# Router logits of three batches from one fp32 sum, added up on GpSimd in two halves of the tokens, in place of TensorE products of two parts

## The chip, the cores and the metric

The kernel runs on one core of one Trainium2 chip. Its time is the time of the device in microseconds (us); lower is better. Engines are named as the profile names them: PE is TensorE (PEld its loading of weights), DVE is VectorE, ACT is ScalarE, POOL is GpSimd, SP is SyncE.

## The reference

A gated block over 4 batches of 512 tokens of width 512: cross attention to 512 context rows of width 128, then a mixture of experts beside a shared network, both on a layer norm of the running x. Everything is fp32.

```python
x = x + tanh(g_xattn[0]) * xattn(layernorm(x), ctx_512, W_k, b_k, ln_gamma, ln_beta)
x = x + tanh(g_ffn[0]) * ffn(layernorm(x), gate_w, e_bias, Wu, Wd, Wsu, Wsd)

def ffn(h, ...):                      # h: 2048 x 512
    logits = h @ gate_w               # 512 x 32: this is what the change is about
    scores = sigmoid(logits)          # then groups, top 2 of 4 groups, top 4 of 32 experts, weights
    ...
    routed = sum over the 4 chosen experts of w * relu2(h @ Wu[e]) @ Wd[e]
    return routed + relu2(h @ Wsu) @ Wsd
```

The logits decide which experts a token gets, so they are computed in full fp32.

## The kernel before

The kernel is written engine by engine, each engine's instructions in an order set by hand, with semaphores between them. There is no scheduler: what stands first on an engine runs first.

The span has a front part (to about 136 us), where attention, the normalised rows `HR` and the shared network's products of the four batches b = 0 to 3 are interleaved; a middle part, where the shared network goes on beside the choice of experts; a loop over 81 expert tiles; and a tail that adds the experts' rows.

What the change touches lies in the front part. For each batch:
- DVE makes `HR` (`h_norm`, L1147) with a reciprocal root that POOL computes (`roots`, L592, an instruction of 128x4). PE turns `HR` (`h_t`, L1963), a tile of 128 tokens at a time.
- ACT copies a turned tile from PSUM into `hT_hi` as fp32r, the high part (L737). DVE subtracts that from the same PSUM tile, which gives `hT_lo`, the low part (`h_low`, L1152).
- The shared network's products (`up_shared`, `down_shared`) are each made of three: high by high, high by low, low by high, in fp32r (L1805).
- The logits (`logits_t`) are fp32 products of `gate` with `hT_hi` and then with `hT_lo`, both added in one PSUM bank. `gate` has 4 blocks of 128 rows by 32 experts, and block h writes its own 32 partitions of the bank, so that the four blocks lie in four column groups of PE. The bank `U[1]` then holds four partial sums; ACT copies it to `lgT`, PE turns that (`logits`, L1997), and DVE adds the four parts up into `LG` (L1160).
- Batch 3 is different: its logits come from the turned fp32 rows themselves. The change leaves it alone.

`U[1]` is shared. The next batch's `out_t` or `ctx_t` writes it, and so waits until DVE has read the logits out of it:

```python
            def out_t(b, js=range(TPB)):
                if js[0] == 0:
                    pe.wait_ge(s["act_kv"], b + 1)
                    if b == 3:
                        pe.wait_ge(s["dve_lg"], 2)
```

In DVE's order `logits(1)` stands behind the last `added` (L1130) and `x2_part` (L1135) of batch 2. DVE's instructions of the attention are `scaled` (L1112), `shifted` (L1118) and `added` (L1130); from batch 2 on `scaled` reads its scores from the SBUF tile `PS`, before that from PSUM. `low_part` (L1178) is the low part of the shared network's activations. POOL's whole list in the front part is its constants, `gam` and `bet`, and eight `roots`, two for each batch.

Of the kernel before, what the change touches and what calls it, by code (L numbers as in the profile page):

```python
# [5 lines left out]
P = 128  # L6
N_BATCH, SEQ, H = 4, 512, 512
DC = 128
TPB = SEQ // P
NT = N_BATCH * TPB  # L10
HB = H // P
E, INNER = 32, 256
# [22 lines left out]
def block_kernel(nc, x, ctx_in, g_xattn, g_ffn, w_k, b_k, ln_gamma, ln_beta,  # L35
                 gate_w, e_bias, w_up, w_down, w_sh_up, w_sh_down, out):
    f32, i32, u32 = mybir.dt.float32, mybir.dt.int32, mybir.dt.uint32
    f16, bf16, f32r = mybir.dt.float16, mybir.dt.bfloat16, mybir.dt.float32r
    ALU, ACT, AX = mybir.AluOpType, mybir.ActivationFunctionType, mybir.AxisListType
    ds = bass.ds  # L40

    with ExitStack() as stack:
        def sb(name, shape, dt=f32):
            return stack.enter_context(nc.sbuf_tensor(name, shape, dt))

        def bank(name):
            return stack.enter_context(nc.psum_tensor(name, [P, 512], f32))

        def sem(name):
            return stack.enter_context(nc.semaphore(name))  # L50
# [13 lines left out]
        gate = sb("gate", [P, HB, E])  # L64
# [56 lines left out]
        def at(name, shape, where, dt=f32):  # L121
            return where.enter_context(nc.sbuf_tensor(name, shape, dt))

        with ExitStack() as front:
            with ExitStack() as ramp:
                out2 = at("out2", [DC, 2, SEQ], ramp)
                key2 = at("key2", [DC, 2, SEQ], ramp)
            hT_hi = at("hT_hi", [P, 2, HB, SEQ], front, f32r)
            hT_lo = at("hT_lo", [P, 2, HB, SEQ], front, f32r)
            wsu_hi = at("wsu_hi", [P, HB, SI], front, f32r)  # L130
            wsd_hi = at("wsd_hi", [P, SB, H], front, f32r)
            spare = at("spare", [P, 2, HB, P], front)
            act_hi = at("act_hi", [P, A_SLOTS, SEQ], front, f32r)
            with ExitStack() as whole:
                wsu = at("wsu", [P, HB, SI], whole)
                wsd = at("wsd", [P, SB, H], whole)
                act = at("act", [P, A_SLOTS, SEQ], whole)
            wsu_lo = at("wsu_lo", [P, HB, SI], front, f32r)
            wsd_lo = at("wsd_lo", [P, SB, H], front, f32r)
            act_lo = at("act_lo", [P, A_SLOTS, SEQ], front, f32r)  # L140
            with ExitStack() as attention:
                ctx_b = at("ctx_b", [P, TPB, DC], attention)
                ctxT = at("ctxT", [DC, SEQ], attention)
                keyT = at("keyT", [DC, SEQ], attention)
                kv = at("kv", [P, TPB, DC], attention)
                PS = at("PS", [P, 2, TPB, SEQ], attention)
                pT = at("pT", [P, TPB, SEQ], attention)
                outT = ctxT
                wk = at("wk", [P, DC], attention)
                wkT = at("wkT", [P, DC], attention)  # L150
                bk = at("bk", [DC, 1], attention)
                gam = at("gam", [P, SEQ], attention)
                bet = at("bet", [P, SEQ], attention)
            with ExitStack() as route:
                with ExitStack() as end:
                    wsd_t = at("wsd_t", [P, SB, H], end)
                wu = at("wu", [P, W_SLOTS, HB, INNER], route)
                wd = at("wd", [P, W_SLOTS, IB, H], route)
                with ExitStack() as weighed:
                    yp2 = at("yp2", [P, 2, H], weighed)  # L160
                sc = at("sc", [P, NT, E], route)
                place = at("place", [P, E, NT], route)
                top_s = at("top_s", [P, NT, 8], route)
                sp_i = at("sp_i", [P, 3, NT, TOPK], route, u32)
                sp_f = at("sp_f", [P, 2, NT, TOPK], route)
                with ExitStack() as choice:
                    sfc = at("sfc", [P, NT, E], choice)
                    pair = at("pair", [P, 2, NT * GROUPS, EG // 2], choice)
                    four = at("four", [P, 4, NT * GROUPS, EG // 4], choice)
                    gsm = at("gsm", [P, 4, NT * GROUPS], choice)  # L170
                    gcmp = at("gcmp", [P, 2, NT, GROUPS, GROUPS], choice)
                    sm = at("sm", [P, NT, E + 4], choice)
                    sm2 = at("sm2", [P, NT, E + 4], choice)
                    top8 = at("top8", [P, NT, 8], choice)
                    chosen = at("chosen", [P, E, NT], choice, bf16)
                    run = at("run", [P, E, NT], choice)
                    incl = at("incl", [P, E, NT], choice)
                    n_i = at("n_i", [P, 2, E], choice, i32)
                with ExitStack() as found:
                    tsum = at("tsum", [P, N_TILES], found)  # L180
                    tpos = at("tpos", [P, TOPK, N_TILES], found)
                    tofs = at("tofs", [P, 2, N_TILES], found)
                with ExitStack() as kept:
                    with ExitStack() as whole:
                        wsu_t = at("wsu_t", [P, HB, SI], whole)
                    wsu_tlo = at("wsu_tlo", [P, HB, SI], kept, f32r)
                    with ExitStack() as matched:
                        yp3 = at("yp3", [P, 2, H], matched)
                    match = at("match", [P, NT // 4, TOPK, E], kept)
                selA = at("selA", [P, NT * TOPK // 2, P], route, f16)  # L190
                selB = at("selB", [P, NT * TOPK // 2, N_TILES], route, f16)
        wu2 = wu[:, :, :, :].rearrange("p s h n -> p (s h n)")
        wd2 = wd[:, :, :, :].rearrange("p s h n -> p (s h n)")
        with ExitStack() as early:
# [78 lines left out]
        U = [bank("U0"), bank("U1")]  # L273
# [29 lines left out]
        def outs_of(b):  # L303
            return out2[:, b, :] if b < 2 else outT[:, :]

        names = """d_x00 d_small d_gate d_tanh d_wk d_bk d_h d_out
            pool_c pool_r dve_c dve_wh pe_bk pe_g act_bk act_th
            dve_v dve_u dve_z dve_e dve_x1 dve_h dve_ws dve_lo dve_sh dve_hT dve_lg dve_ch
            dve_M dve_tab dve_sel dve_tabT dve_idx dve_eact dve_xl dve_el dve_wu dve_wd dve_cmb
            act_c act_ctxT act_kvT act_kv act_pT act_mean act_outT act_ss act_sim act_e act_r act_hT act_lgT act_ws act_sq act_sc  # L310
# [6 lines left out]
        s = {n: sem(n) for n in names}  # L317
# [241 lines left out]
        def _(pool):  # L559
# [29 lines left out]
            def roots(j, n):  # L589

                pool.wait_ge(s["dve_v"], n)
                pool.tensor_tensor(rstd[:, j, :], veps[:, j, :], mhalf[:, :], ALU.pow).then_inc(s["pool_r"], 1)  # L592

            pool.wait_ge(s["d_small"], 16 * 2)
            pool.tensor_scalar(gam[:, :], gam[:, :], -1.0, 0.0, ALU.mult, ALU.add).then_inc(c, 1)
            pool.tensor_scalar(bet[:, :], bet[:, :], -1.0, 0.0, ALU.mult, ALU.add).then_inc(c, 1)
            roots(0, 1)
            roots(1, 2)
            roots(0, 3)
            roots(1, 4)  # L600
            for b in range(2, N_BATCH):
                roots(0, 2 * b + 1)
                roots(1, 2 * b + 2)

            pool.wait_ge(s["dve_tab"], 2)
            used = pool.value_load(used_tab[0:1, 0:1], min_val=NT * TOPK, max_val=N_TILES)
# [1196 lines left out]
        def _(pe):  # L1803
            def mm(o, l, r, start=True, stop=True):
                return pe.matmul(o, l, r, start=start, stop=stop)  # L1805
# [160 lines left out]
            def logits_t(b):  # L1966

                def product(h, rows, start=True, stop=True):

                    return mm(U[1][h * E:(h + 1) * E, :].rearrange("p (t n) -> p t n", n=P), gate[:, h, :], rows,  # L1970
                              start, stop)

                if b == N_BATCH - 1:
                    pe.wait_ge(s["act_tT"], TPB)
                    pe.wait_ge(s["dve_lg"], b)
                    for h in range(HB):
                        i_ = product(h, HR[:, :, h * P:(h + 1) * P])
                    i_.then_inc(s["pe_lgT"], 1)
                    return
                pe.wait_ge(s["act_hT"], TPB * b + TPB)  # L1980
                if b == 0:
                    pe.wait_ge(s["d_gate"], 16 * 2)
                elif b == 1:
                    pe.wait_ge(s["act_mean"], 8)
                else:
                    pe.wait_ge(s["act_outT"], 4)
                pe.wait_ge(s["dve_hT"], TPB * b + TPB)
                for part in (hT_hi, hT_lo):
                    rows_of = part[:, b % 2, :, :].bitcast(f32).rearrange("p h (t n) -> p h t n", n=P)
                    for h in range(HB):  # L1990
                        i_ = product(h, rows_of[:, h, :, :], part is hT_hi, part is hT_lo)
                i_.then_inc(s["pe_lgT"], 1)

            def logits(b):
# [156 lines left out]
            for j in range(2):  # L2151
                i_ = pe.transpose(T[1][0:1, j * P:(j + 1) * P], eid[:, j:j + 1], ident[:, :])
# [169 lines left out]
```

## Time and profile before

| | us |
|---|---|
| median of 3 runs | 545.59 |
| lowest and highest of them | 545.41, 546.27 |
| profiled execution, from its first to its last instruction (span) | 543.3 |
| median less span, which lies around the instructions | 2.3 |
| PE busy | 531.8 (98%) |
| DVE busy | 412.1 (76%) |
| POOL busy | 190.0 (35%) |

No time apart from its span is on record for the profiled execution. The busy shares are means over parts of the kernel with different limits, so they don't say what a microsecond is worth at a given place. The rows of the trace further down do that.

### The profile page before, as it was taken

The numbers are of one execution on the slowest core, as the hardware profiler recorded it, in microseconds if no ns is written. First come the engines' busy times: TensorE is split into PE (matmuls) and PEld (weight loads), VectorE is DVE, ScalarE is ACT, GpSimd is POOL, SyncE is SP. The second block draws the span as 40 slices with busy tenths as digits, with TensorE's granted clock in tenths as the row PEclk, the third lists the DMA queues.
The fourth block names the chain that finished last, engine by engine and source line by source line (L and its number), as shares of the span: only waits on it lengthen the run. The fifth ranks groups of instructions, "written<-read, shape, count | busy, mean of one in ns | idle before, by whom it ended". The sixth has DMA issues, their size and how long they took to land.

```text
span 543.3 us, 11125 instructions
## 1 busy us (share of the span) xinstructions
PE 531.8 (98%) x3090; PEld 434.4 (80%) x3091; DVE 412.1 (76%) x906; ACT 339.5 (62%) x669; POOL 190.0 (35%) x194
## 2 busy tenths in 40 slices
PE   7999999999999999999999999999999999999997
PEld 4555776778788888999999999999999999986553
DVE  4799995494998958666787897777677575756997
ACT  4778673755327855677778787776777776753210
POOL 2110000000000032655657766666656566531000
PEclk9999999999999999999999999999999999999999
DMA  8931012006000024997887988788889778899998
GB/s 311 350 125 39 14 65 77 2 1 210 23 1 0 2 78 151 358 322 222 307 254 237 317 274 254 277 261 275 269 299 316 272 246 268 270 316 358 411 415 328
DMA packets 56393, 116.48 MB, mean 214 GB/s; under 512 B 5493, under 2 KB 24054, under 8 KB 55926
## 3 DMA queue, kind: packets, MB, share of 16 engines
q1 hardware_dynamic: 43200, 72.97, 40.8%
q0 software_dynamic: 12960, 42.48, 21.5%
q8 instruction: 35, 0.57, 0.4%
q14 instruction: 48, 0.39, 0.3%
q10 hardware_dynamic: 150, 0.07, 0.0%
HBM read 85.87 MB, written 29.62 MB: 213 GB/s over the span
## 4 chain that ended last, share of the span: by engine, by line
PE 73%; DVE 14%; DMA 5%; ACT 4%; issue 2%; SPq 1%; DVEq 0%; POOL 0%; ACTq 0%; POOLq 0%
PE U L1805 32%; PE D L1805 28%; PE T L2164 6%; DVE X L1782 5%; PE D L2183 3%; DMA yg<-y_rows 2%; PE T L1805 2%; SPq L508 1%; DVE X L1130 1%; DVE X L1184 1%; DMA y_rows<-yb,idx_s 1%; DVE bst L1135 1%; DMA h_rows<-HR 1%; DVE PS L1118 1%; PE T L1963 1%
## 5 line engine op out<-in xcount | busy, mean ns | idle before, releaser
L618 POOL DMA_INDIRECT xg<-h_rows,idx_g x81 | 88.0, 1086 | 107.9 <-DVE idx_g L1530 70.9
L625 POOL DMA_INDIRECT y_rows<-yb,idx_s x81 | 89.6, 1106 | 81.5 <-ACT yb L935 63.9
L1564 DVE TENSOR_TENSOR xgT_lo<-T,xgT_hi 128x512 fp32r<-128x512 f32 x81 | 56.0, 691 | 48.5 <-ACT xgT_hi L918 48.2
L935 ACT ACTIVATE yb<-D 128x512 f32<-128x512 f32 x81 | 48.7, 602 | 58.2 <-PE D L1805 58.2
L1805 PE MATMUL U<-wu_hi,xgT_hi 128*128 x324 | 58.2, 301 | 0.6 <-DVE xgT_lo L1564 0.6
L1805 PE MATMUL D<-wd_hi,eaT_hi 128*128 x162 | 57.3, 435 | 0.0
L918 ACT ACTIVATE xgT_hi<-T 128x512 fp32r<-128x512 f32 x81 | 48.1, 594 | 10.5 <-issue 8.7
L1805 PE MATMUL U<-wu_hi,xgT_lo 128*128 x324 | 51.8, 282 | 0.0
L1805 PE MATMUL U<-wu_lo,xgT_hi 128*128 x324 | 51.6, 281 | 0.0
L1805 PE MATMUL D<-wd_lo,eaT_hi 128*128 x162 | 50.6, 394 | 0.0
L1805 PE MATMUL D<-wd_hi,eaT_lo 128*128 x162 | 50.1, 391 | 0.0
L2164 PE MATMUL T<-ident,xg 128*128 128x128 f32 x324 | 48.5, 272 | 0.0
L2164 PEld LDWEIGHTS T<-ident,xg 128*128 128x128 f32 x324 | 40.2, 140 | 10.2
L1569 DVE SCALAR_TENSOR_TENSOR eact<-U,erel 128x256 f32<-128x256 f32 x81 | 34.0, 420 | 17.7 <-ACT erel L923 17.3
L1554 DVE TENSOR_TENSOR wu_lo<-wu,wu_hi x32 | 39.2, 1226 | 9.2 <-issue 9.2
L1782 DVE SCALAR_TENSOR_TENSOR X<-yg,w,X 128x512 f32<-128x512 f32 x60 | 40.6, 748 | 5.4 <-DMA yg<-y_rows 5.3
L1805 PEld LDWEIGHTS U<-wu_hi,xgT_hi 128*128 128x128 f32 x324 | 43.9, 190 | 1.0 <-issue 0.8
L1805 PEld LDWEIGHTS U<-wu_hi,xgT_lo 128*128 128x128 f32 x324 | 44.4, 190 | 0.0
L1805 PEld LDWEIGHTS U<-wu_lo,xgT_hi 128*128 128x128 f32 x324 | 44.1, 188 | 0.0
L592 POOL TENSOR_TENSOR rstd<-veps,mhalf 128x4 f32<-128x4 f32 x8 | 8.1, 1013 | 96.1 <-DVE veps L1140 74.8
L1805 PE MATMUL D<-wsd_hi,act_hi 128*128 128x512 f32 x96 | 39.5, 412 | 0.0
L1559 DVE TENSOR_TENSOR wd_lo<-wd,wd_hi x32 | 38.9, 1217 | 0.0
(272 smaller groups left out, 1131.5 us busy)
## 6 DMA issues: line engine op xcount, KB each, us to landing
wu<-in_L_ffn_Wu SPq DMA_DIRECT2D x32, 512.0 KB, 5.0
wd<-in_L_ffn_Wd SPq DMA_DIRECT2D x32, 512.0 KB, 5.3
yg<-y_rows SPq DMA_DIRECT2D x18, 512.0 KB, 10.9
out<-X SPq DMA_DIRECT2D x16, 256.0 KB, 5.9
X<-in_x SPq DMA_DIRECT2D x3, 1024.0 KB, 11.4
h_rows<-HR SPq DMA_DIRECT2D x3, 1024.0 KB, 4.3
yg<-y_rows SPq DMA_DIRECT2D x3, 1024.0 KB, 12.2
wsu<-in_L_ffn_Wsu SPq DMA_DIRECT2D x2, 1024.0 KB, 8.7
```

The source lines that it names most:

```text
L618: pool.indirect_dma_start(out=xg[:, u, :], out_offset=None, in_=h_dram[:, :], in_offset=bass.IndirectOffsetOnAxis(ap=idx_g[:, t:t + 1], ax ...
L625: pool.indirect_dma_start(out=y_dram[:, :], in_=yb[:, u, :], in_offset=None, out_offset=bass.IndirectOffsetOnAxis(ap=idx_s[:, t:t + 1], ax ...
L918: ac.activation(xgT_hi[:, t % 2, :, :], T[t % 2][:, :].rearrange("p (h n) -> p h n", h=HB), ACT.Copy)\
L935: ac.activation(yb[:, t % UNROLL, :], D[2 + t % 2][:, :], ACT.Copy)\
L1554: ve.tensor_tensor(wu_parts[1][:, ds(split_at(v), W_N)], wu2[:, ds(raw_at(v), W_N)], wu_parts[0][:, ds(split_at(v), W_N)].bitcast(f32), AL ...
L1559: ve.tensor_tensor(wd_parts[1][:, ds(split_at(v), W_N)], wd2[:, ds(raw_at(v), W_N)], wd_parts[0][:, ds(split_at(v), W_N)].bitcast(f32), AL ...
L1564: ve.tensor_tensor(xgT_lo[:, t % 2, :, :], T[t % 2][:, :].rearrange("p (h n) -> p h n", h=HB), xgT_hi[:, t % 2, :, :].bitcast(f32), ALU.su ...
L1569: ve.scalar_tensor_tensor(eact[:, t % 2, :], U[t % 2][:, 0:INNER], 0.0, erel[:, t % 2, :], ALU.max, ALU.mult).then_inc(s["dve_eact"], 1)
L1782: ve.scalar_tensor_tensor(X[:, t, :], row_at(t, k), w4[:, t * TOPK + k:t * TOPK + k + 1], X[:, t, :], ALU.mult, ALU.add).then_inc(s["dve_c ...
L1805: return pe.matmul(o, l, r, start=start, stop=stop)
L2164: i_ = pe.transpose(T[t % 2][:, h * P:(h + 1) * P], xg[:, t % UNROLL, h * P:(h + 1) * P], ident[:, :])
L2183: i_ = pe.transpose(D[t % 2][:, k * P:(k + 1) * P], eact[:, t % 2, k * P:(k + 1) * P], ident[:, :])
```

## The change

For batches 0 to 2 POOL adds `hT_hi` and `hT_lo` up again, a tile of 128 tokens at a time, into a new fp32 tensor. The first two tiles of a batch go to `hT_0`, which takes the place of an unused buffer of the same size, the last two to `hT_1`, in memory of the attention. PE then multiplies `gate` with that sum: for each half of 256 tokens it waits for the two adds of that half and runs 4 products (one for each block h) of 256 columns. Before, it ran 8 products of 512 columns for the batch.

```diff
-            spare = at("spare", [P, 2, HB, P], front)
+            hT_0 = at("hT_0", [P, HB, 2 * P], front)
...
+                hT_1 = at("hT_1", [P, HB, 2 * P], attention)
...
+            def h_whole(b):
+
+                if b:
+                    pool.wait_ge(s["pe_lgT"], b)
+                for it in range(TPB):
+                    pool.wait_ge(s["dve_hT"], TPB * b + it + 1)
+                    cols = slice(it * P, (it + 1) * P)
+                    pool.tensor_tensor(hT_whole[it // 2][:, :, it % 2 * P:(it % 2 + 1) * P],
+                                       hT_hi[:, b % 2, :, cols].bitcast(f32), hT_lo[:, b % 2, :, cols].bitcast(f32),
+                                       ALU.add).then_inc(s["pool_h"], 1)
+
             roots(0, 1)
             roots(1, 2)
             roots(0, 3)
+            h_whole(0)
             roots(1, 4)
-            for b in range(2, N_BATCH):
-                roots(0, 2 * b + 1)
-                roots(1, 2 * b + 2)
+            roots(0, 5)
+            h_whole(1)
+            roots(1, 6)
+            roots(0, 7)
+            h_whole(2)
+            roots(1, 8)
...
-                pe.wait_ge(s["act_hT"], TPB * b + TPB)
...
-                pe.wait_ge(s["dve_hT"], TPB * b + TPB)
-                for part in (hT_hi, hT_lo):
-                    rows_of = part[:, b % 2, :, :].bitcast(f32).rearrange("p h (t n) -> p h t n", n=P)
+                for half in range(2):
+                    pe.wait_ge(s["pool_h"], TPB * b + 2 * half + 2)
                     for h in range(HB):
-                        i_ = product(h, rows_of[:, h, :, :], part is hT_hi, part is hT_lo)
+                        i_ = mm(U[1][h * E:(h + 1) * E, half * 2 * P:(half + 1) * 2 * P], gate[:, h, :],
+                                hT_whole[half][:, h, :])
```

On PE this is the place in batch 1, between the turning of the keys of batch 3 and that of its x; before the change:

```order
L1852 MATMUL T<-ident,keyT 128x128 x4
L1805 MATMUL U<-hT_hi,gate 32x512 x4
L1805 MATMUL U<-hT_lo,gate 32x512 x4
L1879 MATMUL T<-ident,X 128x128 x8
L1805 MATMUL D<-wsd_hi,act_hi 128x512
```

and of the changed kernel, whose lines are 17 further down:

```order
L1869 MATMUL T<-ident,keyT 128x128 x4
L1822 MATMUL U<-hT,gate 32x256 x8
L1896 MATMUL T<-ident,X 128x128 x8
L1822 MATMUL D<-wsd_hi,act_hi 128x512
L1822 MATMUL D<-wsd_lo,act_hi 128x512
```

The number of products stays at eight, each has half the columns, and nothing else has moved on PE. DVE, ACT and SP keep their order too.

POOL's list, from its constants to its first gather of expert rows (`pool_r` counts its roots, and `[waits ...]` names what a row waits for), is before the change:

```order
L595 TENSOR_SCALAR gam<-gam 128x512 [waits d_small]
L596 TENSOR_SCALAR bet<-bet 128x512
L592 TENSOR_TENSOR rstd<-veps,mhalf 128x4 [waits dve_v] x8
L606 TENSOR_LOAD used_tab [waits dve_tab]
L606 ISA x2
```

and of the changed kernel:

```order
L597 TENSOR_SCALAR gam<-gam 128x512 [waits d_small]
L598 TENSOR_SCALAR bet<-bet 128x512
L594 TENSOR_TENSOR rstd<-veps,mhalf 128x4 [waits dve_v] x3
L606 TENSOR_TENSOR hT<-hT_hi,hT_lo 128x4x128 [waits dve_hT] x4
L594 TENSOR_TENSOR rstd<-veps,mhalf 128x4 [waits dve_v] x2
L606 TENSOR_TENSOR hT<-hT_hi,hT_lo 128x4x128 [waits dve_hT,pe_lgT]
L606 TENSOR_TENSOR hT<-hT_hi,hT_lo 128x4x128 [waits dve_hT] x3
L594 TENSOR_TENSOR rstd<-veps,mhalf 128x4 [waits dve_v] x2
L606 TENSOR_TENSOR hT<-hT_hi,hT_lo 128x4x128 [waits dve_hT,pe_lgT]
L606 TENSOR_TENSOR hT<-hT_hi,hT_lo 128x4x128 [waits dve_hT] x3
L594 TENSOR_TENSOR rstd<-veps,mhalf 128x4 [waits dve_v]
```

Twelve adds of 128x512 elements, each with two SBUF inputs, now stand between the third and the last of the eight roots.

## Rows read from the trace of the kernel before

**Rows 1.** The page, busy time of two engines: us, share, instructions

```profile
PE 531.8 (98%) x3090; PEld 434.4 (80%) x3091; DVE 412.1 (76%) x906; ACT 339.5 (62%) x669; POOL 190.0 (35%) x194
```

**Rows 2.** Busy time in four stretches, in the order PE, PEld, DVE, ACT, POOL

```profile
39.37:65.17 25.80, 24.00 (x119) 16.53 (x117) 24.71 (x49) 20.15 (x38) 1.83 (x2) 1.00 0.11 41
65.17:86.92 21.75, 21.75 (x136) 17.41 (x136) 21.26 (x55) 13.68 (x29) 1.01 (x1) 1.00 0.13 49
86.92:112.45 25.53, 25.53 (x110) 18.26 (x112) 12.53 (x31) 14.45 (x30) 2.01 (x2) 1.00 0.12 42
112.45:136.31 23.86, 23.43 (x121) 18.07 (x121) 16.01 (x41) 13.34 (x23) 1.01 (x1) 1.00 0.37 127
```

**Rows 3.** The chain that ended last, 40 to 66 us: start, us, what

```profile
43.74 0.69 DVE PS L1118
...
44.47 0.81 ACT PS L731 x2
...
48.93 2.29 DVE wsd_lo L1173
...
64.56 0.56 DVE HR L1147
65.12 0.04 issue
65.17 1.11 PE T L1963 x8
```

**Rows 4.** The same chain, 112 to 137 us

```profile
112.47 0.61 ACT act L723
...
125.22 0.56 DVE HR L1147
...
125.79 4.50 DMA h_rows<-HR
```

**Rows 5.** Timeline of PE: start, us, what, idle before

```profile
77.51 1.07 PE L1805 MATMUL U<-hT_hi,gate 128*32 128x512 f32 x8
78.39 1.04 PE L1805 MATMUL U<-hT_lo,gate 128*32 128x512 f32 x8
79.36 1.09 PE L1879 MATMUL T<-ident,X 128*128 128x128 f32 x8
...
87.14 3.59 PE L1805 MATMUL U<-pT,kv 128*128 128x512 f32 x8
...
112.36 1.06 PE L1805 MATMUL U<-hT_hi,gate 128*32 128x512 f32 x8
...
136.31 1.06 PE L1805 MATMUL U<-HR,gate 128*32 128x512 f32 x8 [0.43 <-ACT HR L745]
```

**Rows 6.** Timeline of DVE in batch 1

```profile
69.95 1.42 DVE L1112 SCALAR_TENSOR_TENSOR PS<-PS,rstd,gam 128x512 f32<-128x512 f32 x2
...
72.50 1.28 DVE L1152 TENSOR_TENSOR hT_lo<-T,hT_hi 128x512 fp32r<-128x512 f32 x2
...
74.08 0.75 DVE L1130 SCALAR_TENSOR_TENSOR X<-PS,ecoef,X 128x512 f32<-128x512 f32 x1
...
86.25 0.67 DVE L1160 TENSOR_REDUCE LG<-U 128x128 f32<-128x512 f32 x1
```

**Rows 7.** Timeline of DVE in batch 2

```profile
103.59 1.29 DVE L1152 TENSOR_TENSOR hT_lo<-T,hT_hi 128x512 fp32r<-128x512 f32 x2 [1.59 <-ACT hT_hi L737]
104.79 1.41 DVE L1112 SCALAR_TENSOR_TENSOR PS<-PS,rstd,gam 128x512 f32<-128x512 f32 x2
...
110.91 1.28 DVE L1152 TENSOR_TENSOR hT_lo<-T,hT_hi 128x512 fp32r<-128x512 f32 x2
...
114.43 0.69 DVE L1178 TENSOR_TENSOR act_lo<-act,act_hi 128x512 fp32r<-128x512 f32 x1 [0.44 <-ACT act L727]
```

**Rows 8.** Timeline of POOL

```profile
3.01 0.29 POOL L582 CAST iota_f<-iota_i 128x128 f32<-128x128 int32 x1
...
20.31 0.61 POOL L596 TENSOR_SCALAR bet<-bet 128x512 f32<-128x512 f32 x1
...
39.19 1.01 POOL L592 TENSOR_TENSOR rstd<-veps,mhalf 128x4 f32<-128x4 f32 x1 [2.72 <-DVE veps L1101]
```

More of the change, by code:

```diff
@@ L191, in block_kernel @@
                 selB = at("selB", [P, NT * TOPK // 2, N_TILES], route, f16)
+        hT_whole = (hT_0, hT_1)
         wu2 = wu[:, :, :, :].rearrange("p s h n -> p (s h n)")
@@ L306, in block_kernel @@
         names = """d_x00 d_small d_gate d_tanh d_wk d_bk d_h d_out
-            pool_c pool_r dve_c dve_wh pe_bk pe_g act_bk act_th
+            pool_c pool_r pool_h dve_c dve_wh pe_bk pe_g act_bk act_th
             dve_v dve_u dve_z dve_e dve_x1 dve_h dve_ws dve_lo dve_sh dve_hT dve_lg dve_ch
```

## The prediction

> **What bounds the kernel now.** I read the page first: PE is busy 98% of the span, DVE 76% [rows 1]. That invites the thought that any work taken off PE is time saved, so I looked next at the chain that ended last and at busy time by stretches. The reader is to see that in the front part PE's 98% is not a bound everywhere. From 39.37 to 65.17 us DVE is busy 24.71 of 25.80 us and PE has gaps [rows 2]; the chain runs through DVE and ACT (shifted scores at 43.74, their exponential on ACT at 44.47, the low part of the weights at 48.93, the normalised rows at 64.56) and PE is released at 65.17 by those rows [rows 3]. From 65.17 to 86.92 both are full: PE 21.75 of 21.75, DVE 21.26 of 21.75. From 86.92 to 112.45 PE is full and DVE half idle: here PE alone sets the pace. From 112.45 to 136.31 neither is [rows 2]: the chain leaves PE at 112.47 for ACT, goes over DVE to the rows at 125.22 and a transfer of 4.50 us [rows 4], and PE has run out of work 0.43 us before it is released at 136.31 [rows 5]. From there on PE is full again, and whatever shift the front part has is handed to the end.
>
> **What the change removes.** In batch 1 the two groups of gate products begin at 77.51 and 78.39 and the next work at 79.36 [rows 5]: 1.85 us for 8 products, which the trace records as 16. Half the columns should give about half, 0.93 us, if the columns set the time; nothing, if the loading of 16 sets of weights does. I take 0.9 us a batch, 2.7 us in all, with 0 as the lower bound. None of it ends up at the end as it stands:
> - Batch 0: PE is released at 65.17 by DVE [rows 3]. PE's gain only makes that gap longer. Worth 0.
> - Batch 1: behind the gate products come 7 us of full PE, and then `out_t(3)` at 87.14 [rows 5], which waits for DVE to have read the logits of batch 1 out of the bank `U[1]`. That instruction stands at 86.25 for 0.67 us, to 86.92 [rows 6], on a DVE that had nothing but work since 65.17 [rows 2]. With 0.05 us for the signal (as from 65.12 to 65.17 [rows 3]) PE can be 87.14 - 86.97 = 0.17 us earlier, not 0.9. Worth 0.17.
> - Batch 2: the chain leaves PE at 112.47 [rows 4], and the gate products of batch 2 stand at 112.36 [rows 5], behind what it needs from PE. PE's gain again lengthens the gap of 0.43 us. Worth 0.
>
> **What it adds.** Twelve adds on POOL. No row shows a POOL add of two tensors of this size. From below: one input of 128x512 takes 0.61 us and 128x128 takes 0.29 us [rows 8], so 0.83 ns for each of the 512 elements of a partition and 0.18 us fixed. If the two inputs and the output never overlap, three times the element cost: 0.18 + 3 x 0.43 = 1.5 us. I take two times, 0.18 + 2 x 0.43 = 1.04, say 1.1 us with its wait, since it is nearest in kind to the one-input row with one operand more. The Trainium skill (GPSIMD Engine Reference, Performance versus the Vector engine) has 4497 ns for an add of 2048 elements; a quarter is 1.12 us.
>
> Is an add ready when PE wants it? Batch 0: POOL is done with its root at 39.19 + 1.01 = 40.20 [rows 8], the four adds end at 44.6, and the gate products stood just there; PE's gap before 65.17 covers what is missing. Batch 1: the last `hT_lo` ends at 73.8 [rows 6], the adds by 76, before 77.51. Batch 2: `hT_lo` of the last two tiles ends at 111.6 and 112.2 [rows 7]; the adds run 111.55 to 112.65 and to 113.75, so PE's second half starts 1.4 us after 112.36 and ends at about 114.3, as late as it did before. That costs nothing.
>
> **What it disturbs.** The adds run exactly while DVE runs instructions with two SBUF inputs of 128x512, and DVE is the chain in batches 0 and 1 and again after 112.47. No row of before has a POOL instruction of this kind beside such a DVE instruction, so the price of a meeting is unknown: from below 0; from above the whole add, 1.1 us, if only one of the two can read at a time. I exclude a gain: nothing leaves DVE. I take the upper end, one waits while the other runs: both are engines that stream a whole tile from SBUF without a pause, and there is no third case in between for which a row speaks. With that:
> - Batch 0: the adds run 40.2 to 44.6 at 1.1 each. The DVE instruction at 43.74 has two SBUF inputs [rows 3] and meets the fourth, which began at 43.5: 0.86 us late. It stands on the chain (ACT at 44.47, DVE at 48.93, rows at 64.56 [rows 3]), so 0.86 goes on. As an add may also end just before it, the bounds are 0.1 and 1.1.
> - Batch 1: adds 1 and 2 are free to start at 69.95, as is the first of a row of four two-input instructions (two at 69.95 [rows 6]). If the engines take turns, DVE waits for an add after each of the first two: 2.2. The two `hT_lo` at 72.50 read PSUM and one SBUF tile and wait for nobody. Add 3 then costs the X update (74.08 before, now 76.28) 0.1 and add 4 the one behind it 1.1: 3.4 in all. If instead DVE holds what it has while it runs back to back, the adds begin beside `hT_lo` at 72.50; the second ends at 74.7 and costs the X update 0.6, and the two others catch one each, 0.6 and 0.7: 1.9 to 2.0. `out_t(3)` then waits for the logits' reading at 86.25 [rows 6] by 3.4 or 2.0, less the 0.17.
> - Batch 2: add 1 runs 104.2 to 105.3 and holds up the instruction at 104.79 [rows 7] by 0.5, add 2 the next one by 1.1, or in the other order a later one by 0.6. `hT_lo` at 110.91 and the adds behind it move along, and add 4 holds up the last shift by 0.4. That is 2.0 or 1.5, of which 0.44 us of DVE's idle time before 114.43 [rows 7] covers a part: 1.6 or 1.1. From 114.43 on DVE is on the chain. PE's gate products are late by as much, but PE has its 0.43.
>
> **The sum.** In turns 0.86 + 3.4 - 0.17 + 1.6 = 5.7 us; DVE first 0.86 + 2.0 - 0.17 + 1.1 = 3.8 us. I take the middle, 4.7 us. On the span: 543.3 + 4.7 = 548.0, and with 2.3 around it 550.3 us; the 2.3 is the median less the span, so the sum is made against the median of 545.59 at the same time.
>
> The rule behind the choice is the Trainium skill's (SBUF — State Buffer, Who interferes with whom): GpSimd's only read port is VectorE's second one, a VectorE instruction with two SBUF inputs contends with a GpSimd instruction that reads SBUF, and whichever began first holds it to its end. By that rule the meetings cost what I summed; a reader who doesn't trust it has the rival below. No row here shows it either way.
>
> **The rivals.**
> 1. *The two engines don't disturb each other* (ends on the other side: not slower). The place is DVE between 40 and 87 us, the price 0 a meeting. Then 0 + 0.17 + 0 is saved: 545.4 us, within what can be told from no change. It decides if a meeting costs less than about 0.2 us, as there are some seven of them. For it: the root at 39.19 [rows 8] reaches into the stretch in which DVE is busy 24.71 of 25.80 us [rows 2], so a POOL instruction beside DVE doesn't stop it as such; but that one has 4 elements. Chance 0.26.
> 2. *Only the adds are late.* DVE goes first always, element by element, or an add takes nearer 1.5 to 1.9 us. At 1.9 the adds of batch 2 end at 111.55 + 3.8 = 115.35, PE's second half ends at 115.8 where it ended at 114.2, and 1.6 - 0.43 = 1.2 us go to the end: 546.8. In between lie meetings that cost a part of an add, up to +3 us: 546.6 to 548.6. Chance 0.12.
> 3. *PE's saving comes through.* If the waits I named weren't there, 2.7 us of 545.59: 542.9. Against it speaks DVE's 21.26 of 21.75 us [rows 2] in front of `out_t(3)`. Chance 0.04.
> 4. *The forecast,* 3 to 6.5 us slower. Chance 0.58.
>
> **How the numbers follow.** About 0.2% (1.1 us) is what a measurement of this kernel can tell from no change. Slower by more: the forecast and nearly all of rival 2, 0.69. Within: rival 1 and a rest of 2, 0.27. Faster: rival 3, 0.04. The forecast's own range is 548.6 to 552.0. The range for 8 in 10 has to take in rival 1 from 545.3 and leaves out rival 3 and the rare cases above 551.8, where every meeting costs a whole add.
>
> **What would show it.** In the changed profile: an add on POOL of about 1.1 us, start to start; the gate products of a batch in about 0.95 us; DVE instructions with two SBUF inputs (L1112 on PS, L1118, L1130, L1178) of 1.5 to 1.8 us where one lies beside an add, or a gap before them, and `hT_lo` and the statistics unchanged; the logits' reading of batch 1 at 89 to 91 us in place of 86.25, with PE waiting for it; PE's gate products with HR at 140 to 142 us in place of 136.31. From there the difference stays. I am wrong if those DVE instructions keep their 0.7 us and their starts: then the time is 545.4. I am wrong in size if adds take another time or always fall into DVE's one-input instructions.

## The result

The changed kernel is slower: 551.49 us, median of 5 runs (550.65 to 552.69), against 545.59 (545.41 to 546.27). The ratio is 1.0115, with a 95% interval of 1.0102 to 1.0128, so about 6 us are lost. 550.3 us had been forecast, 4.7 us more than before; it became 5.9. Ratios here are worked out from the single executions, without those more than 1.5% above the fastest of their kernel, and can differ by 0.1% from the quotient of two medians.

The span of the profiled execution is 550.7 us, 7.4 more than before. To see where they arise I divide the front part at three instructions of PE. A is the start of the turning of `HR` of batch 1, B the way from there to `out_t(3)`, C the way from there to the gate products with `HR`. A profiled execution is one run, and for this kernel it can differ by 1 to 2 us from the median, so A, B and C say where, and the medians how much.

| us | A | B | C |
|---|---|---|---|
| before [rows 3, 5] | 65.17 | 21.97 | 49.17 |
| changed | 65.32 | 26.18 | 52.37 |
| difference | +0.15 | +4.21 | +3.20 |

C is 49.17 us before, and 48.66 and 48.73 in kernels 2 and 3 below, whose batch 2 is as before, so half a microsecond in C says little. Together the differences are 7.56 us: the gate products with `HR` start at 143.87 for 136.31 [rows 5], and from there to the end of the span it is 406.8 us for 407.0. Behind C nothing is added. Batch 0 costs next to nothing, batch 1 makes B longer, batch 2 makes C longer.

**What POOL does.** Its adds in the timeline of the changed kernel (start, us, what, idle before and who ended it):

```profile
40.22 5.48 POOL L606 TENSOR_TENSOR hT<-hT_hi,hT_lo 128x512 f32<-128x512 f32 x4
...
70.03 2.99 POOL L606 TENSOR_TENSOR hT<-hT_hi,hT_lo 128x512 f32<-128x512 f32 x2
...
75.48 2.51 POOL L606 TENSOR_TENSOR hT<-hT_hi,hT_lo 128x512 f32<-128x512 f32 x2 [2.45 <-DVE hT_lo L1169]
...
108.75 3.00 POOL L606 TENSOR_TENSOR hT<-hT_hi,hT_lo 128x512 f32<-128x512 f32 x2 [1.34 <-DVE hT_lo L1169]
...
117.57 2.50 POOL L606 TENSOR_TENSOR hT<-hT_hi,hT_lo 128x512 f32<-128x512 f32 x2 [5.82 <-DVE hT_lo L1169]
```

An add takes 1.25 us (2.51 for two), and 1.5 where two of them take turns with DVE's longer instructions. 1.1 had been put in. The fourth add of batch 0 by itself:

```profile
43.97 1.73 POOL L606 TENSOR_TENSOR hT<-hT_hi,hT_lo 128x512 f32<-128x512 f32 x1
```

It is 0.48 us longer than 1.25, and DVE's two-input instruction at 43.80, below, has lost only 0.07. Here POOL is the one that waited.

**What DVE does.** Its timeline in batches 0 to 2, to set beside [rows 3], [rows 6] and [rows 7]:

```profile
43.80 0.76 DVE L1135 CUSTOM_DVE_ANT_0 PS<-PS,bet 128x512 f32<-128x512 f32 x1
...
70.10 3.48 DVE L1129 SCALAR_TENSOR_TENSOR PS<-PS,rstd,gam 128x512 f32<-128x512 f32 x2
...
74.72 1.27 DVE L1169 TENSOR_TENSOR hT_lo<-T,hT_hi 128x512 fp32r<-128x512 f32 x2
...
76.10 0.66 DVE L1143 TENSOR_TENSOR ecoef<-esum,g_tanh 128x1 f32<-128x1 f32 x1
76.80 1.74 DVE L1147 SCALAR_TENSOR_TENSOR X<-PS,ecoef,X 128x512 f32<-128x512 f32 x1
...
78.45 0.68 DVE L1135 CUSTOM_DVE_ANT_0 PS<-PS,bet 128x512 f32<-128x512 f32 x1
...
89.94 0.67 DVE L1177 TENSOR_REDUCE LG<-U 128x128 f32<-128x512 f32 x1
...
109.12 3.17 DVE L1129 SCALAR_TENSOR_TENSOR PS<-PS,rstd,gam 128x512 f32<-128x512 f32 x2
```

The reader is to see which rows have grown. The pair of two-input instructions at 70.10 takes 3.48 us for 1.42 [rows 6], while two adds stand beside it on POOL. The X update takes 1.74 for 0.75. Even an instruction of one element for each partition, `ecoef`, takes 0.66 us; before it took 0.16:

```profile
73.89 0.16 DVE L1126 TENSOR_TENSOR ecoef<-esum,g_tanh 128x1 f32<-128x1 f32 x1
```

Those three make 2.06 + 0.99 + 0.50 = 3.55 us, which with the 0.15 of A accounts for the 3.69 by which the logits' reading moves, from 86.25 to 89.94. `hT_lo`, which takes one of its inputs from PSUM, keeps its time: 1.27 for 1.28 [rows 6].

**What PE does.** Its timeline at the places of [rows 5], with the two waits that are new:

```profile
80.61 1.12 PE L1869 MATMUL T<-ident,keyT 128*128 128x128 f32 x4 [2.02 <-ACT keyT L706]
81.66 1.94 PE L1822 MATMUL U<-hT,gate 128*32 128x256 f32 x16
...
91.50 3.59 PE L1822 MATMUL U<-pT,kv 128*128 128x512 f32 x8
...
116.69 0.64 PE L1822 MATMUL U<-hT,gate 128*32 128x256 f32 x8
...
120.12 0.64 PE L1822 MATMUL U<-hT,gate 128*32 128x256 f32 x8 [2.80 <-POOL hT L606]
...
143.87 1.06 PE L1822 MATMUL U<-HR,gate 128*32 128x512 f32 x8
```

Two things weren't in the forecast. In batch 1 PE waits 2.02 us already at the keys, far ahead of `out_t(3)`. It waits there for ACT's copy of the keys (`keyT`), which stands behind an exponential that waited for DVE, as ACT's timeline shows:

```profile
79.17 0.72 ACT L748 ACTIVATE PS<-PS,nmax 128x512 f32<-128x512 f32 x1 [2.50 <-DVE nmax L1135]
79.89 0.67 ACT L706 ACTIVATE keyT<-T,kmean 128x512 f32<-128x512 f32 x1
```

And after each of the two idle times PE runs slower. Stretches of the changed kernel, columns as in [rows 2]; the eighth number, behind POOL's, is the granted clock:

```profile
65.17:80.60 15.43, 12.30 (x72) 10.19 (x72) 15.29 (x31) 7.30 (x17) 6.48 (x5) 1.00 0.18 68
80.60:83.50 2.90, 2.88 (x20) 1.31 (x20) 2.83 (x7) 2.84 (x6) 0.00 (x0) 0.50 0.03 6
...
116.70:120.10 3.40, 0.63 (x9) 0.14 (x8) 3.40 (x6) 1.86 (x3) 2.50 (x2) 1.00 0.00 0
...
121.30:125.20 3.90, 3.90 (x12) 3.03 (x11) 2.79 (x7) 1.47 (x5) 0.00 (x0) 0.56 0.00 0
```

From 80.60 to 83.50 the granted clock is 0.50, its 1.2 GHz level, and the gate products take 1.94 us. From 121.30 to 125.20, behind 2.80 us of idle time, it is 0.56 in the mean.

### The profile page after: what moved, and what is told of

Read it like the earlier page. It is cut to its first block, busy times and chain, and to the rows that moved or that the text cites. A ratio compares the mean times of both kernels' runs of the same rounds, so it can differ in the third digit from the quotient of the medians.

```text
span 550.7 us, 11139 instructions
## 1 busy us (share of the span) xinstructions
PE 533.2 (97%) x3090; PEld 436.2 (79%) x3091; DVE 418.2 (76%) x906; ACT 339.7 (62%) x669; POOL 206.8 (38%) x206
## 4 chain that ended last, share of the span: by engine, by line
PE 83%; DVE 11%; ACT 3%; issue 1%; DMA 1%; POOL 0%; DVEq 0%; ACTq 0%
PE U L1822 35%; PE D L1822 34%; PE T L2180 6%; PE D L2199 3%; DVE PS L1129 2%; PE T L1822 2%; DVE X L1147 1%; DVE hT_lo L1169 1%; DVE PS L1135 1%; DVE bst L1106 1%; DVE act_lo L1195 1%; DVE bst L1152 1%; ACT PS L748 1%; PE T L1896 1%; DMA wk<-in_L_xattn_W_k 1%
## 5 line engine op out<-in xcount | busy, mean ns | idle before, releaser
L740 ACT ACTIVATE act<-U 128x512 f32<-128x512 f32 x23 | 13.7, 596 | 41.3 <-PE U L1822 41.3
```

## The experiments

Two theories at first. *Turns*: a POOL instruction that reads SBUF and a DVE instruction with two SBUF inputs never run together, each waits for the whole of the other, and DVE's lost time is the loss. *Late adds*: PE waits for sums that come too late, and DVE's longer rows are an accident beside it. After the first four kernels (1 to 4) a third question came up: what the clock adds. Those four ran on a chip on which the kernel before took 554.68 us (549.36 to 557.40 in 35 executions), 5 to 8 beside 545.17, and 9 to 11 beside 545.07. Only the comparison with before on the same chip is read.

**1. The adds without their user.** POOL adds as in the change, PE computes its logits as before it.

```diff
             def h_whole(b):
-                if b:
-                    pool.wait_ge(s["pe_lgT"], b)
...
-            pe.wait_ge(s["pool_h"], TPB * b + 2 * half + 2)   # and the 4 products of a half
+            # the 8 products with hT_hi and hT_lo, as before
```

POOL no longer waits for PE, and ACT waits for the adds of batch 0 before it overwrites `hT_hi` in batch 2; they are done 60 us earlier.

> The adds run on POOL where the changed kernel has them, but PE computes the logits as before the change and waits for no add; nothing else differs from the kernel before. Theory (a DVE instruction with two SBUF inputs waits for a whole add): the pair of L1112 in batch 1 takes about 3.5 us in place of 1.4, the logits of batch 1 are read 3.5 to 3.7 us late, and the kernel is at least 4 us slower than before (549.5 to 553). Rival (the cost is PE waiting for adds, and DVE's long instructions in the changed kernel come from PE being late): nothing waits for an add, so 545.4 to 546.0 and L1112 as before.

560.63 us, median of nine executions (that of all twelve is 561.44), against 554.68, ratio 1.0111 (1.0073 to 1.0150): the whole loss, though no instruction of PE waits for POOL. B is 27.17 us, C 50.16; behind PE's wait for the keys the granted clock is 0.50 here too (82 to 85 us). The pair on DVE and PE's gate products of batch 2:

```profile
70.57 3.47 DVE L1129 SCALAR_TENSOR_TENSOR PS<-PS,rstd,gam 128x512 f32<-128x512 f32 x2
```

```profile
119.62 1.06 PE L1822 MATMUL U<-hT_hi,gate 128*32 128x512 f32 x8 [1.41 <-DVE hT_lo L1169]
```

PE waits here too, for a `hT_lo` that DVE delivers late. That the sums are late for PE isn't needed for a loss of this size. The adds on POOL are enough, through DVE.

**2 to 4. One batch at a time.** `h_whole(b)` and the new products for one batch only; shown for batch 1:

```diff
-            h_whole(0)
...
             h_whole(1)
...
-            h_whole(2)
...
+                if b != 1:
+                    # the 8 products with hT_hi and hT_lo, as before
```

> Only batch 0 is changed. Theory: its adds meet one large DVE instruction and PE has slack, so 545.5 to 545.9, no difference that can be told. Rival (every batch costs a third of the 5.9 us): 547.5.

> Only batch 1 is changed. Theory: DVE late by 3.7 us, PE late by the same through the keys of batch 3, PE's clock halved for about 3 us after its gap, nothing regained from the halved columns: 4.0 to 4.6 us slower, 549.6 to 550.2. Rival (clock alone, or batch 2 alone, is the cost): under 2 us, 547.5 or less.

> Only batch 2 is changed. Theory: PE waits some 2.8 us for the last add, then runs 3 to 4 us at half clock, less the 0.43 us of slack: 2.5 to 3.3 us slower, 548.1 to 548.9. Rival (as I predicted: DVE's chain alone decides): 1.1 to 1.6 us slower, 546.7 to 547.2, and no drop of the granted clock.

| | median | ratio (95%) | A | B | C |
|---|---|---|---|---|---|
| batch 0 only | 554.89 | 1.0005 (0.9972 to 1.0038) | 66.16 | 21.97 | 48.66 |
| batch 1 only | 558.21 | 1.0066 (1.0030 to 1.0102) | 64.94 | 25.40 | 48.73 |
| batch 2 only | 558.06 | 1.0071 (1.0036 to 1.0106) | 65.21 | 21.98 | 53.59 |

Batch 0 costs nothing that can be told, as expected. The other two cost 3.6 and 3.9 us (0.66% and 0.71% of about 550), where 4.0 to 4.6 and 2.5 to 3.3 were expected. Their sum of 7.5 us is over the 6 us of the whole, but each has an interval of about 2 us either way.

The A of 66.16 is not batch 0's price. This execution was already 0.88 us late at the root on POOL that stands ahead of the adds (39.19 before [rows 8]):

```profile
40.07 1.01 POOL L594 TENSOR_TENSOR rstd<-veps,mhalf 128x4 f32<-128x4 f32 x1 [2.72 <-DVE veps L1116]
```

From the start of that root to A it takes 26.05 to 26.09 us in the six profiles with the adds of batch 0, and 25.98 to 26.01 in the six with nothing of POOL's there, before among them. Batch 0 costs 0.1 us. In the kernel with batch 1 alone PE waits just as long at the keys as in the changed kernel, but keeps its clock:

```profile
80.23 0.66 PE L1867 MATMUL T<-ident,keyT 128*128 128x128 f32 x4 [2.02 <-ACT keyT L704]
80.82 1.07 PE L1820 MATMUL U<-hT,gate 128*32 128x256 f32 x16
```

In the one with batch 2 alone it does not. Its stretches with the wait and behind it:

```profile
112.38:115.74 3.36, 0.64 (x10) 0.15 (x9) 3.36 (x6) 1.86 (x3) 2.49 (x2) 0.92 0.00 0
115.74:122.00 6.26, 6.26 (x20) 4.32 (x21) 3.97 (x10) 2.11 (x5) 0.00 (x0) 0.50 0.00 0
```

**5. The saving without the adds.** Products of half the columns, but of `hT_hi` alone; the low part is left out of the logits of batches 0 to 2.

```diff
-            h_whole(0)                       # and (1) and (2)
...
-                    pe.wait_ge(s["pool_h"], TPB * b + 2 * half + 2)
+                    pe.wait_ge(s["dve_hT"], TPB * b + 2 * half + 2)
...
-                                hT_whole[half][:, h, :])
+                                hT_hi[:, b % 2, h, half * 2 * P:(half + 1) * 2 * P].bitcast(f32))
```

> No adds: PE multiplies the gate with the high part alone, in the two halves, so the low part's share of the logits is left out. This shows what the shorter products are worth by themselves. Theory: the products of a batch take 0.9 to 1.0 us in place of 1.85, and all but 0.17 us of it is lost in waits for DVE: 545.2 to 545.7. Rival (PE's saving comes through): 542.8.

545.16 us against 545.17, ratio 1.0004 (0.9994 to 1.0014). PE's timeline in batch 1:

```profile
77.93 1.07 PE L1819 MATMUL U<-hT_hi,gate 128*32 128x256 f32 x16
78.94 0.66 PE L1893 MATMUL T<-ident,X 128*128 128x128 f32 x4
80.03 0.66 PE L1893 MATMUL T<-ident,X 128*128 128x128 f32 x4 [0.44 <-ACT kv L707]
...
87.44 3.67 PE L1819 MATMUL U<-pT,kv 128*128 128x512 f32 x8
```

From their start to that of the next work the products take 1.01 us, where they took 1.85 [rows 5]. PE then waits 0.44 us for ACT, and B is 21.85 us, 0.12 less than before.

**6. One input for POOL.** POOL copies `hT_hi` in place of adding; again the low part is left out of the logits.

```diff
-                    pool.tensor_tensor(hT_whole..., hT_hi..., hT_lo..., ALU.add)
+                    pool.tensor_scalar(hT_whole..., hT_hi..., 1.0, 0.0, ALU.mult, ALU.add)
```

> POOL copies the high part (one SBUF input) in place of adding the two, so the low part is left out of the logits; all waits are those of the changed kernel. Theory (whichever reads first holds the other off for its whole length, and one input is enough): a copy takes about 0.6 us, each meeting costs at most that, and DVE is late by 1.2 to 2 us in batch 1; 546.8 to 548.5. Rival (only an add of two inputs gets in DVE's way): DVE's instructions keep their 0.7 us and the time is 545.2 to 545.8.

546.23 us against 545.17, ratio 1.0021 (1.0012 to 1.0031): 1.1 us, clear of no change and below the 546.8 to 548.5 expected. DVE's timeline and POOL's:

```profile
70.65 2.12 DVE L1129 SCALAR_TENSOR_TENSOR PS<-PS,rstd,gam 128x512 f32<-128x512 f32 x2
...
75.29 0.60 DVE L1143 TENSOR_TENSOR ecoef<-esum,g_tanh 128x1 f32<-128x1 f32 x1
```

```profile
70.59 1.64 POOL L606 TENSOR_SCALAR hT<-hT_hi 128x512 f32<-128x512 f32 x2
...
74.67 1.22 POOL L606 TENSOR_SCALAR hT<-hT_hi 128x512 f32<-128x512 f32 x2 [2.43 <-DVE hT_lo L1169]
```

One SBUF input on POOL's side is enough to hold DVE up, and the shorter instruction on POOL costs less: the pair on DVE loses 0.70 us to copies of 0.61, and 2.06 to adds of 1.25.

**7. Batch 2's gate products later.** So that PE doesn't stand idle for POOL, `logits_t(2)` goes behind `down_shared(7)`.

```diff
-            logits_t(2)
             down_shared(7)
+            logits_t(2)
```

> The changed kernel with the gate products of batch 2 behind the next down_shared on PE, 2.7 us of work that does not need the adds. Theory (PE's wait of 2.8 us for the last add and the halved clock behind it make up most of batch 2's share, but DVE's lateness stays): no wait, clock 1.00 there, 1.0 to 2.5 us faster than the changed kernel, 549.0 to 550.5. Rival (DVE's lateness alone carries batch 2): as the changed kernel, 551.5.

PE's gate products take 1.29 us, start to start, so 0.3 us of wait at most; its clock in batch 2 is 1.00, and C is 50.23 us, 1.06 more than before in place of 3.20. What holds PE up now are rows that come late over DVE and ACT, before with 0.43 us [rows 5]:

```profile
142.18 1.06 PE L1822 MATMUL U<-HR,gate 128*32 128x512 f32 x8 [1.06 <-ACT HR L762]
```

The median is 551.25 against 545.17, ratio 1.0122 (1.0105 to 1.0138): the forecast gain of 1.0 to 2.5 us is not there.

**8. The idle time filled.** To part the clock from the wait, PE repeats earlier gate products into columns that are already final before it waits; the repeated work is added to the computation.

```diff
+                    if b == 2 and half:
+                        for n in range(6 * HB):
+                            h = n % HB
+                            mm(U[1][h * E:(h + 1) * E, 0:2 * P], gate[:, h, :], hT_whole[0][:, h, :])
                     pe.wait_ge(s["pool_h"], TPB * b + 2 * half + 2)
```

> The changed kernel, in which PE repeats the first half's products of batch 2 six more times (about 2.8 us of work without use) before it waits for the last adds. The wait is as long as before, but PE is busy in it. Theory (the idle time itself makes the clock fall): granted clock 1.00 after it, the 12 products behind it take 2.8 us in place of 4.5, and 1.2 to 1.8 us are gained on the changed kernel: 549.7 to 550.3. Rival (the clock falls for another reason, or DVE's chain decides anyway): 551.5.

Stretches with the filled wait and behind it:

```profile
117.55:121.01 3.46, 3.23 (x58) 1.72 (x57) 3.46 (x6) 1.86 (x3) 2.53 (x2) 1.00 0.00 0
121.01:124.43 3.42, 3.42 (x21) 2.52 (x21) 3.35 (x10) 1.30 (x3) 0.00 (x0) 1.00 0.02 5
```

PE still gets its sums when POOL has them (121.01), but the clock stays at 1.00, and the next 12 products take 2.85 us (121.58 to 124.43), not the 4.45 of the changed kernel (120.69 to 125.14). C is 50.77 us, +1.60: half of the 3.20 is the clock's. The median again doesn't follow. It is 554.08 against 545.17, ratio 1.0156 (1.0134 to 1.0178), where 549.7 to 550.3 had been expected.

**9. The changed kernel again,** on the chip of kernels 10 and 11, with no edit.

> The changed kernel again, on the chip and in the session of the others, to see whether the clock falls at the same places. Theory (DVE's delays and PE's waits are fixed by the program, the fall of the clock is not): DVE's pair of L1129 again 3.4 to 3.5 us, PE's waits again 2.0 and 2.7 to 2.8 us, the halved clock in other stretches or absent, ratio 1.010 to 1.013. Rival (the clock is fixed by the program as well): half clock again at 81 to 84 and 121 to 125 us.

552.42 us against 545.07, ratio 1.0143 (1.0123 to 1.0164). The ratio is above the 1.010 to 1.013 expected. A, B, C are 64.87, 25.40, 52.47, and DVE's pair of L1129 takes 3.48 us again. Here the clock doesn't fall in batch 1, but does in batch 2:

```profile
80.17:83.50 3.33, 3.27 (x31) 2.18 (x32) 3.26 (x7) 3.27 (x7) 0.00 (x0) 1.00 0.02 5
...
120.50:124.50 4.00, 4.00 (x12) 3.09 (x12) 2.76 (x8) 1.12 (x3) 0.00 (x0) 0.57 0.00 0
```

and so PE comes to `out_t(3)` in time to be held up by the logits' reading, which ends at 90.17, as the prediction had it:

```profile
90.27 3.67 PE L1822 MATMUL U<-pT,kv 128*128 128x512 f32 x8 [0.26 <-issue]
```

```profile
89.50 0.67 DVE L1177 TENSOR_REDUCE LG<-U 128x128 f32<-128x512 f32 x1
```

**10, 11. The whole rows without POOL.** For batches 1 and 2 ACT copies the turned rows a second time, in fp32; batch 0 is left as it was before the change. PE's products are those of the change. In the first version DVE also reads the logits of batch 1 earlier, ahead of `added(2, 3)` and `x2_part(2, 3)`; in the second it doesn't. DVE makes `hT_lo` of a tile only after ACT's second copy of it.

```diff
+                    ac.activation(hT_whole[it // 2][:, :, it % 2 * P:(it % 2 + 1) * P],
+                                  h_bank(b, it)[...], ACT.Copy).then_inc(s["act_w"], 1)
...
-                    pe.wait_ge(s["pool_h"], TPB * b + 2 * half + 2)
+                    pe.wait_ge(s["act_w"], TPB * (b - 1) + 2 * half + 2)
```

> A try at a version that beats both. Batch 0 as before the change. In batches 1 and 2 ACT copies the turned rows a second time from PSUM, as fp32, in place of POOL's adds, and PE multiplies the gate with them in the two halves. DVE reads the logits of batch 1 ahead of the last attention update of batch 2, so that out_t of batch 3 waits less for it. Theory (POOL's reads were the whole harm, and with the wait for the logits moved PE's saving of 0.9 us in batch 1 gets through): DVE's instructions keep 0.7 us, 0.6 to 0.9 us faster than before, 544.3 to 544.6 where before is 545.2. Rival (the extra copies make ACT and hT_lo late, and the 0.9 us are lost again): same as before or up to 0.5 us slower.

> As the run with ACT's copies, but the logits of batch 1 are read where they were. Theory (PE is held to 0.17 us by that reading): 0 to 0.2 us faster than before, 545.0 to 545.2 where before is 545.2, and PE waits some 0.7 us for the reading ahead of out_t of batch 3. Rival (the reading was never the limit): as fast as the run with the reading moved.

545.23 and 545.95 us against 545.07: ratios 1.0008 (0.9993 to 1.0023) and 1.0020 (1.0009 to 1.0031). Both expectations, of 0.6 to 0.9 and 0 to 0.2 us gained, failed. In the first, the reading has moved up and yet `out_t(3)` stands where it stood:

```profile
84.67 0.69 DVE L1171 TENSOR_REDUCE LG<-U 128x128 f32<-128x512 f32 x1
```

```profile
79.80 0.66 PE L1890 MATMUL T<-ident,X 128*128 128x128 f32 x4 [0.42 <-ACT kv L696]
...
87.15 3.59 PE L1816 MATMUL U<-pT,kv 128*128 128x512 f32 x8
```

PE's saved time now goes into waits for ACT. With the shorter products in batches 1 and 2 and no POOL add, the loss is gone but for 0.2% in the second version, and nothing is gained. None of the versions beats the kernel before.

## Why the prediction was right in its direction and short in its size

- **The mechanism was right.** POOL and DVE take turns. The adds alone bring the whole loss (1.0111 beside 1.0115), and the shorter products without POOL bring none (1.0004). So rival 2, that only the adds are late, is out too. The Trainium skill (SBUF — State Buffer, Who interferes with whom) says that whichever of the two began holds the read port to its end. The traces agree: 3.48 us for 1.42 with two adds in between, and rival 1, no disturbance, is out.
- **Saving: right.** 0.17 us were put in, 0.12 measured with the adds taken away. PE's 98% busy wasn't its worth; that is the part of rival 3, and it is out. One reason was missing: beside DVE, ACT too holds PE up as soon as it is earlier (0.44 and 0.42 us).
- **The add: 1.25 us, not 1.1,** inside the bounds of 1.04 and 1.5.
- **Batch 0: 0.86 us put in, 0.1 found** (26.05 to 26.09 us from the root on POOL to A, for 25.98 to 26.01). An add of 1.25 us instead of 1.1 shifts the start of the fourth from 43.5 to 43.97, so that DVE's instruction came in ahead of it: the lower of the two cases named. A meeting that a shift of 0.3 us decides shouldn't have stood in the sum at nearly its full price.
- **Batch 1: 3.4 less 0.17 put in, 3.4 found** where the clock stays up (B is 25.40 in two kernels). The choice between the two variants was open; it is turns, 3.48 us for the pair. That the pair on DVE took another 2.06 us fits 2.2. Of the rest, the meeting with `ecoef`, an instruction of 128x1, wasn't named: I had listed only those of 128x512. The reading ends late and `out_t(3)` waits for it, as predicted. In the first profile that wait is hidden: the low clock behind the keys brings PE to `out_t(3)` 0.8 us later still.
- **Batch 2: 1.6 or 1.1 put in, 3.20 in the profile. This is the step that failed:** "PE's second half starts 1.4 us after 112.36 and ends at about 114.3, as late as it did before. That costs nothing." The adds were counted from the `hT_lo` of before. But the paragraph on what the adds disturb has DVE 1.5 to 2 us later, and the two weren't put together. DVE's pair at 109.12 is 1.76 us late, two adds are 0.3 us longer, and PE, whose wait should have been 0.75 us by the prediction's starts, waits 2.80. With PE's 0.43 us of slack off, that gives the 1.60 us that C is longer by in the kernel with the filled wait. At full clock the size put in was therefore met, but partly by luck: with PE's wait taken out (kernel 7) DVE's lateness alone leaves 1.06.
- **The clock: not in the sum at all, the other half of the same step.** Behind the wait of 2.80 us, 12 products take 4.45 us (120.69 to 125.14) for 2.85: the other 1.6 us of C. That repeating products in the gap takes this away, and that there is no fall in kernel 7 either, where PE hardly waits, points to the idle time as the cause. But the fall doesn't follow every such wait. The same 2.02 us at the keys are followed by a clock of 0.50 to 0.55 in four profiles (changed, 1, 7, 8), and by 1.00 in two (changed again, batch 1 alone). In batch 2 it fell in all three profiles of that wait left as it is (2.72 to 2.80 us), and not behind the 1.41 us of kernel 1.
- The middle between the two variants, 4.7 us, was also a choice. It took 0.7 us off batch 1's 3.4, and the 0.76 too much in batch 0 made up for that: luck. With turns throughout, the prediction's own 5.7 us would have met the median's 5.9, and that would have been luck as well, with too much in batch 0 and no clock.

**How much of the median is the clock's.** The start of PE's gate products with `HR` (A + B + C), and what is left of the span behind it:

| us | start | span | behind it | median of its runs, ratio |
|---|---|---|---|---|
| before | 136.31 | 543.3 | 407.0 | 1 |
| changed | 143.87 | 550.7 | 406.8 | 1.0115 |
| changed, again | 142.74 | 549.7 | 407.0 | 1.0143 |
| 7, logits later | 142.18 | 549.0 | 406.8 | 1.0122 |
| 8, time filled | 143.13 | 552.5 | 409.4 | 1.0156 |

Kernels 7 and 8 gain 2.1 and 1.6 us in C over the first profile of the changed kernel, but their A and B, which their edits don't touch, are together 1.7 and 2.1 us longer than in the second. That is a later start ahead of the adds and a fall of the clock at the keys, so only the fall in batch 2 was taken away.

Every execution has its mean granted clock on record. The first profile of the changed kernel, with two falls, has 0.994, the second, with one, 0.997. Its ten executions on two chips, on which the kernel before takes 545.59 and 545.07 us:

| mean granted clock | executions | us |
|---|---|---|
| 0.999 | 1 | 550.65 |
| 0.996 to 0.997 | 4 | 550.92 to 551.58 |
| 0.994 | 4 | 552.42 to 553.50 |
| 0.991 | 1 | 554.33 |

The kernel before shows 0.997 to 1.000 on the second of these chips. So of the first median's 5.9 us some 5.1 are there without the clock, by the one execution at 0.999, and some 0.8 come with it; that is an estimate. The three batches at full clock give the same: 0.1 + 3.4 + 1.6 = 5.1. The ratio of 1.0143 belongs to five executions of 0.997 and less. The four executions of kernel 7 lie at 0.996 and 0.997 and take 550.84 to 552.65 us, as much as the changed kernel at that clock: PE's wait for the adds was worth little by itself, 0.5 us in C (50.77 less 50.23).

**What stays open.** Why the same idle time is followed by the low clock in some executions only. Kernel 8 also loses 2.4 us behind the front part; 2.2 of them are one wait of PE at 504.43, in the tail, and why it is there wasn't tried. And no POOL instruction that only writes SBUF was run beside DVE, so the runs show that an instruction that reads one or two tiles holds DVE up, and not whether every one does.

## What to carry to other kernels

Before a POOL instruction is placed in a stretch where DVE is on the chain, count DVE's instructions with two SBUF inputs there, small ones too: each meeting costs up to POOL's whole instruction. A copy by ACT out of PSUM did the same job without that, though here it won nothing either. And when an edit delays both the inputs of the added instructions and those instructions themselves, add the two delays up before PE's wait is worked out, and price an idle PE of 2 to 3 us at more than its length (here up to 1.6 us on top).

## What the runs showed of the hardware that I had not expected

- A DVE instruction of 128x1 with two SBUF inputs took 0.66 us beside a POOL instruction, 0.16 without.
- POOL is held up as well: two adds took 2.51 us where only DVE waited and 2.99 in turns, two copies 1.22 and 1.64.
- The fp32 gate products of a batch, 16 records either way, took 1.01 us with 256 columns and 1.85 us with 512, start to start, so the columns set the time there and not the loading of weights.
- The granted clock went to 0.50 for 3 to 6 us after PE had been idle for 2.0 to 2.8 us, in some executions only. Executions with a mean granted clock of 0.994 took 1.8 to 2.9 us more than the one at 0.999.
